# First layer of a two-layer decoder on one core: lag products moved to ScalarE, rounding to VectorE, and a selection loop without instructions that read two SBUF tensors

## The reference, cut to what matters

```python
def reference(x, ctx_768, masks, weights):           # x (2,512,128), ctx (2,154,96)
    # layer 0, gated recurrence, then a cross attention that steers a state-space filter
    x = layernorm(x + attn0(x))
    Q, K, V = (x @ Wq), (ctx @ Wk), (ctx @ Wv)         # 4 heads of 32
    scores = einsum('bthd,bghd->bhtg', Q, K) / sqrt(32)          # 154 keys
    topv, topi = top_k(scores, 32)
    attn = zeros_like(scores).at[..., topi].set(softmax(topv))
    c_t = attn.mean(heads) @ V * text_mask
    scale_in, shift_in   = split(c_t @ W_film_in  + b_film_in)
    scale_out, shift_out = split(c_t @ W_film_out + b_film_out)
    u = layernorm(x) * (1 + gate * scale_in) + gate * shift_in
    # filter taps of 512 lags: K[d,l] = 2 Re sum_n dC[d,n] exp(dt A[d,n] l), 64 states n
    y = irfft(rfft(u) * rfft(K)) + u * D_skip
    y = y * (1 + gate * scale_out) + gate * shift_out
    x = layernorm(x + y + ffn(layernorm(x + y)))
    # layer 0 experts, then layer 1 (attention of 16 heads, cross attention, experts): not touched
```

## Time and profile before

| what | value |
| --- | --- |
| median of 3 runs | 851.5 us (851.27 to 851.51) |
| the profiled execution: its own time | 854.57 us |
| its span, first to last instruction | 852.7 us |
| busy in the span: PE, DVE, ACT, POOL | 732.2, 491.8, 274.5, 241.7 us |
| mean granted TensorE clock | 0.914 of full speed |

### The profile page before, as it was taken

One profiled execution on the slowest core, in us unless ns is written; L12 is line 12 of the kernel. 1 busy time (PEld: TensorE's weight loads), 2 busy tenths in 40 slices (PEclk: granted clock), 3 DMA queues, 4 the chain that ended last, 5 costly groups with the idle time before them and its releaser, 6 DMA issues.

```text
span 852.7 us, 8489 instructions
## 1 busy us (share of the span) xinstructions
PE 732.2 (86%) x3088; PEld 370.2 (43%) x3088; DVE 491.8 (58%) x1200; ACT 274.5 (32%) x483; POOL 241.7 (28%) x138
## 2 busy tenths in 40 slices
PE   7533556888999899999999999998996999999996
PEld 4211324548568453332222222222843244556555
DVE  7699976804405358656676776764465455332333
ACT  6446645320020210135444444443021402221220
POOL 4881750100001000205554545465071500000000
PEclk9756678987977989999999999999997989999999
DMA  7100004000200000000000000000050000000000
GB/s 293 29 0 0 0 0 172 28 1 1 98 1 1 0 1 0 2 0 1 1 0 1 1 0 1 1 0 1 1 210 0 1 1 0 1 1 0 1 1 25
DMA packets 3491, 18.64 MB, mean 22 GB/s; under 512 B 887, under 2 KB 2040, under 8 KB 2938
## 3 DMA queue, kind: packets, MB, share of 16 engines
q1 hardware_dynamic: 3450, 18.11, 5.6%
HBM read 17.58 MB, written 0.52 MB: 21 GB/s over the span
## 4 chain that ended last, share of the span: by engine, by line
PE 67%; DVE 20%; ACT 6%; issue 3%; POOL 3%; POOLq 0%; DVEq 0%; ACTq 0%
PE PS L1849 9%; PE PS L1332 7%; PE PS L1863 5%; DVE SB L1486 5%; PE PS L1316 4%; PE PS L1287 4%; PE PS L218 3%; PE PS L1300 2%; PE PS L707 2%; DVE SB L1235 2%; PE PS L1348 2%; PE PS L972 2%; PE PS L1370 2%; PE PS L1415 2%; PE PS L1647 2%
## 5 line engine op out<-in xcount | busy, mean ns | idle before, releaser
L198 POOL TENSOR_TENSOR SB<-SB 128x4 f32<-128x4 f32 (+1 forms) x24 | 23.9, 998 | 376.3 <-DVE SB L182 376.2
L1469 POOL TENSOR_TENSOR SB<-SB 128x1024 f32<-128x1024 f32 x32 | 75.3, 2354 | 127.6 <-ACT SB L1439 127.5
L1486 DVE TENSOR_REDUCE SB<-PS 128x2 f32<-128x1024 f32 x64 | 78.5, 1226 | 52.7 <-PE PS L1300 52.6
L1439 ACT ACTIVATE SB<-PS 128x1024 f32<-128x1024 f32 x64 | 65.6, 1026 | 105.2 <-PE PS L1319 105.1
L218 PE MATMUL PS<-SB 128*128 128x512 f32 (+1 forms) x190 | 87.3, 606 | 8.3 <-ACT SB L541 6.8
L1849 PE MATMUL PS<-SB 128*128 128x512 f32 x176 | 82.5, 607 | 0.0
L1316 PE MATMUL PS<-SB 64*128 64x512 f32 x256 | 68.9, 615 | 0.0
L1332 PE MATMUL PS<-SB 128*64 128x512 f32 x256 | 67.8, 610 | 1.2 <-DVE SB L1523 1.2
L1519 DVE RECIPROCAL SB<-PS 128x512 f32<-128x512 f32 x16 | 53.7, 3358 | 17.6 <-PE PS L1348 17.6
L1929 DVE TENSOR_TENSOR SB<-SB,PS 128x512 f32<-128x512 f32 (+1 forms) x48 | 32.9, 689 | 52.7 <-PE PS L1849 48.8
L1863 PEld LDWEIGHTS PS<-SB 128*128 128x128 f32 (+1 forms) x384 | 49.3, 190 | 18.6 <-issue 10.1
(11 more groups left out here) (359 smaller groups left out, 1219.4 us busy)
## 6 DMA issues: line engine op xcount, KB each, us to landing
SB<-exp SPq DMA_DIRECT2D x1, 4352.0 KB, 13.8
SB<-moe SPq DMA_DIRECT2D x1, 4096.0 KB, 12.9
SB<-dft SPq DMA_DIRECT2D x1, 2304.0 KB, 11.6
SB<-att SPq DMA_DIRECT2D x1, 2048.0 KB, 7.9
SB<-mix SPq DMA_DIRECT2D x1, 768.5 KB, 4.6
SB<-mix SPq DMA_DIRECT2D x1, 640.0 KB, 5.7
SB<-ssm SPq DMA_DIRECT2D x1, 602.0 KB, 6.7
SB<-lat SPq DMA_DIRECT2D x1, 585.0 KB
```

What stands on the lines that cost most here:

```text
L1439: act.activation(expd[i % 2][:, 1024 * u:1024 * u + 1024], bank(2 * (u % 2), 2), ACT.Exp).then_inc(sem("d_exp"), 1)
L1469: pool.tensor_tensor(half_sums[half], e[:, 0:1024], e[:, 1024:], ALU.add).then_inc(sem("d_half_sum"), 1)
L1486: dve.tensor_reduce(shift[i % 2][:, qt:qt + DK + 1:DK], two_heads(bank(4, 2)), AX_X, ALU.max, negate=True)\
```

## The change

- **Lag products.** `low_r` and `high_r` are no longer made by two large GpSimd multiplications but by 32 and 16 ScalarE activations, one for each lag (scale = the lag; the low ones add the quarter turn as bias).
- **Rounding** is one VectorE instruction each for the low and the high turns (+ MAGIC, - MAGIC), which replaces L429, two GpSimd passes (L436, L437) and ScalarE's two passes of L517.
- **Selection.** The negated maximum is a TENSOR_REDUCE with negate in place of a TENSOR_TENSOR; the last MATCH_REPLACE8 of a head writes to PSUM (banks 2, 3), so that `selected` reads one operand from there; VectorE makes only 1 / sum, and the mask multiplication moves to ScalarE at the head of `diagonals`.
- **Scores** of all tiles go to banks 0 and 1, each once the tile before is copied; PE issues them three tiles ahead of the gather.
- **Order on ScalarE.** FiLM inputs move behind the first exponentials, low rates to tile 0, high and low sines into one block in tile 2, the copies of the taps to tile 6 (TAPS_AT 4 to 5), the spectrum to tile 7. `normed_again` (8 activations) becomes one GpSimd multiplication.
- **Taps' transform** on PE directly behind gather and FiLM of tile 5, into banks 0 and 1, once all scores are copied.

```diff
-    def b_pool_turns(pool, follow):
-        pool.wait_ge(sem("s_stack_in"), 1)
-        pool.tensor_tensor(lag(low_r, LOW), every(turn_T, LOW), lags(ssm["low_lags"], LOW), ALU.mult).then_inc(sem("s_low_products"), 1)
+    def b_act_low_turns(act, a, z):
+        for l in range(a, z):
+            ins = act.activation(lag(low_r, LOW)[:, :, l], turn_T, ACT.Identity, scale=float(l), bias=ssm["quarter"])
+        if z == LOW:
+            ins.then_inc(sem("s_low_products"), 1)
+    def b_act_high_turns(act, a, z):
+        for l in range(a, z):
+            ins = act.activation(lag(high_r, HIGH)[:, :, l], turn_T, ACT.Copy, scale=float(LOW * l))
+        if z == HIGH:
+            ins.then_inc(sem("s_high_turns"), 1)
...
+    def b_dve_rounds(dve):
         dve.wait_ge(sem("s_low_products"), 1)
-        dve.tensor_scalar(low_k, low_r, ssm["quarter"], MAGIC, ALU.add, ALU.add).then_inc(sem("s_low_rounds"), 1)
+        dve.tensor_scalar(low_k, low_r, MAGIC, MAGIC, ALU.add, ALU.subtract).then_inc(sem("s_rounds"), 1)
+        dve.wait_ge(sem("s_high_turns"), 1)
+        dve.tensor_scalar(high_t, high_r, MAGIC, MAGIC, ALU.add, ALU.subtract).then_inc(sem("s_rounds"), 1)
-    def b_pool_high_turns(pool, follow):
-        follow(pool.tensor_tensor(lag(high_r, HIGH), every(turn_T, HIGH), lags(ssm["high_lags"], HIGH), ALU.mult))
-        m = magic[:, 0:1].to_broadcast([P, 2048])
-        pool.wait_ge(sem("a_out"), 2)
-        follow(pool.tensor_tensor(high_t, high_r, m, ALU.add))
-        follow(pool.tensor_tensor(high_t, high_t, m, ALU.subtract))
+    def b_pool_high_angles(pool):
+        pool.wait_ge(sem("s_rounds"), 2)
         pool.tensor_tensor(high_t, high_t, high_r, ALU.subtract).then_inc(sem("s_high_turns"), 1)
...
     def b_act_pre(act):
-        b_act_low_rates(act, 0, 8)
+        b_act_low_turns(act, 0, 24)
         for h in range(H_X):
             act.wait_ge(sem("x_inputs"), h + 1)
...
-        b_act_low_rates(act, 8, 12)
+        b_act_low_turns(act, 24, LOW)
+        b_act_high_turns(act, 0, 10)
+        act.wait_ge(sem("x_half_turned"), 1)
+        act.activation(xsT[:, 0:512], bank(4), ACT.Copy).then_inc(sem("x_half_in"), 1)
+        b_act_high_turns(act, 10, HIGH)
+        act.wait_ge(sem("turned"), 1)
+        act.activation(xsT[:, 512:], bank(5), ACT.Copy).then_inc(sem("turned_in"), 1)
...
-    TAPS_AT = 4
+    TAPS_AT = 5
...
         def score(t):
-            if t >= 2:
-                pe.wait_ge(sem("x_scores_in"), t - 1)
-            else:
-                pe.wait_ge(sem("x_small_in"), (2, 6)[t])
+            if t >= 1:
+                pe.wait_ge(sem("x_scores_in"), t)
...
-                o = bank(2 * (t % 2) + g)[:, 0:2 * S2]
+                o = bank(g)[:, 0:2 * S2]
...
         def peak(j):
-            dve.tensor_tensor(minus_max[:, 2 * j:2 * j + 2], peaks.rearrange("p (i m) -> p i m", m=8)[:, 2 * j:2 * j + 2, 0],
-                              minus_one, ALU.mult).then_inc(sem("x_minus_max"), 1)
+            dve.tensor_reduce(minus_max[:, 2 * j:2 * j + 2], peaks[:, 16 * j:16 * j + 16].rearrange("p (i m) -> p i m", m=8),
+                              AX_X, ALU.max, negate=True).then_inc(sem("x_minus_max"), 1)
...
-                    ins = dve.match_replace(left[i % 4], m8[k][:, 8 * r:8 * r + 8], left[i % 4], 0.0)
+                    to = rest[:, S2 * k:S2 * k + S2] if r == 3 else left[i % 4]
+                    ins = dve.match_replace(to, m8[k][:, 8 * r:8 * r + 8], left[i % 4], 0.0)
...
-                              left_ring[:, S2 * (i % 4):S2 * (i % 4) + 2 * S2], ALU.subtract).then_inc(sem("x_probs"), 1)
+                              bank(2 + j % 2)[:, 0:2 * S2], ALU.subtract).then_inc(sem("x_probs"), 1)
...
-            follow(dve.reciprocal(a, sums))
-            dve.tensor_tensor(a, a, text_mask[:, t:t + 1].to_broadcast([P, H_X]), ALU.mult).then_inc(sem("x_share"), 1)
+            dve.reciprocal(sums, sums).then_inc(sem("x_sums"), 1)
...
     def b_act_attention(act):
...
         exponentials(0)
+        b_act_film_inputs(act)
         exponentials(1)
-        b_act_low_whole(act)
+        b_act_film_rows(act)
         for t in range(NT):
             if t >= 1:
                 diagonals(t - 1)
+            if t == NT - 1:
+                b_act_spectrum(act)
             if t + 1 < NT:
                 exponentials(2 * t + 2)
             if t + 2 < NT:
                 scores_in(t + 2)
+            if t == 0:
+                b_act_low_rates(act, 0, 16)
+            if t == 2:
+                b_act_high_waves(act)
+                b_act_low_waves(act)
+            if t == TAPS_AT + 1:
+                b_act_taps(act)
             if t + 1 < NT:
                 exponentials(2 * t + 3)
-            if t == TAPS_AT + 1:
-                b_act_taps(act)
             if t >= 1:
                 attn_in(act, t - 1)
                 for k in FILMS[t - 1]:
                     film_in(k)
             if t == 0:
-                b_act_low_rates(act, 20, LOW)
-            if t == 1:
-                b_act_high_waves(act)
-            if t == 2:
-                b_act_low_waves(act)
+                b_act_low_rates(act, 16, LOW)
             if t == 3:
                 b_act_high_rates(act)
-                normed_again()
-            if t == 6:
-                b_act_spectrum(act)
```

More of the change, by code:

```diff
@@ L477, in b_act_spectrum @@
         w = lambda j: ssm["bin_weight"][:, j:j + 1]
-        for out, i in ((taps_re, 6), (taps_im2, 7), (taps_re2, 6)):
+        for out, i in ((taps_re, 0), (taps_im2, 1), (taps_re2, 0)):
             for j in range(4):
@@ L510, in b_act_high_rates @@
         ins.then_inc(sem("s_rates"), 1)
[L512 to L517, removed]
     def b_act_high_waves(act):
-        act.wait_ge(sem("s_high_turns"), 1)
+        act.wait_ge(sem("s_high_turns"), 2)
         act.activation(high_r, high_t, ACT.Abs).then_inc(sem("s_high_waves"), 1)
@@ L530, in b_act_low_waves @@
             act.wait_ge(sem("s_low_products"), h + 2)
-            act.activation(low_k[:, c], low_k[:, c], ACT.Sin, scale=-TWO_PI, bias=ssm["quarter_angle"])\
+            act.activation(low_k[:, c], low_k[:, c], ACT.Sin, scale=-TWO_PI)\
                .then_inc(sem("s_low_waves"), 1)
@@ L724, in film_tile, with taps_spectrum @@
                       stop=True).then_inc(sem("x_film"), 1)
+        def taps_spectrum():
+            pe.wait_ge(sem("x_scores_in"), NT)
+            pe.wait_ge(sem("s_taps_in"), 1)
+            pe.wait_ge(sem("dft_in"), 16)
+            for part, mat in ((0, dft["dft_cos"]), (1, dft["dft_sin"])):
+                for j in range(4):
+                    for c in range(4):
+                        ins = pe.matmul(bank(part)[:, 128 * j:128 * j + 128],
+                                        mat[:, 512 * c + 128 * j:512 * c + 128 * j + 128],
+                                        taps[:, 128 * c:128 * c + 128], start=(c == 0), stop=(c == 3))
+            ins.then_inc(sem("s_taps_dft"), 1)
         score(0)
         score(1)
+        score(2)
         for t in range(NT):
-            if t + 2 < NT and t < TAPS_AT:
-                score(t + 2)
+            if t + 3 < NT:
+                score(t + 3)
             if t == TAPS_AT:
-                score(t + 2)
-                score(t + 3)
                 taps_of_lags()
@@ L744, in b_pe_attention @@
                 film_tile(k)
-            if t == 5:
-                pe.wait_ge(sem("x_film_in"), 5)
-                pe.wait_ge(sem("s_taps_in"), 1)
-                pe.wait_ge(sem("dft_in"), 16)
-                for part, mat in ((0, dft["dft_cos"]), (1, dft["dft_sin"])):
-                    for j in range(4):
-                        for c in range(4):
-                            ins = pe.matmul(bank(6 + part)[:, 128 * j:128 * j + 128],
-                                            mat[:, 512 * c + 128 * j:512 * c + 128 * j + 128],
-                                            taps[:, 128 * c:128 * c + 128], start=(c == 0), stop=(c == 3))
-                ins.then_inc(sem("s_taps_dft"), 1)
+            if t == TAPS_AT:
+                taps_spectrum()
         pe.wait_ge(sem("s_u_late"), 1)
@@ L781, in select @@
             base = 12 * j
+            rest = bank(2 + j % 2)[:, 0:2 * S2]
             if j >= 2:
@@ L850, in diagonals @@
         def diagonals(t):
+            act.wait_ge(sem("x_sums"), 2 * t + 2)
+            act.activation(share[:, H_X * t:H_X * t + H_X], total[:, H_X * t:H_X * t + H_X], ACT.Copy, scale=text_mask[:, t:t + 1])\
+               .then_inc(sem("x_share"), 1)
             act.wait_ge(sem("x_share"), t + 1)
@@ L862, in film_in @@
             act.activation(film[:, 512 * t:512 * t + 512], bank(6 + t % 2), ACT.Copy).then_inc(sem("x_film_in"), 1)
-        def normed_again():
-            act.wait_ge(sem("u_scaled"), 1)
-            for t in range(NT):
-                ins = act.activation(tiled(u_n)[:, t, :], tiled(xs)[:, t, :], ACT.Copy, scale=u_scale[:, t:t + 1])
-            ins.then_inc(sem("u_normed"), 1)
         scores_in(0)
```

45 lines of the change are left out of this document (18 added, 27 removed).

## The result

The kernel after takes **799.8 us** median (798.87 to 800.62, 4 executions) against 851.5 (851.27 to 852.36) before: ratio 0.9391, 95% interval 0.9374 to 0.9407. The profiled execution took 798.87, its span 797.0 us, at a mean granted clock of 0.947 (0.914 before).

A forecast was written before the change was run, and what follows sets the result against it. It took the chain through VectorE, ScalarE and PE up to the last FiLM copy as the bound; gains 13.6 + 12.9 + 12.4 = 38.9 take 854.57 to 815.7, less 3.1 for the median: 812.6 us, range 803 to 824.

The forecast's parts named there:

- Locks: VectorE against GpSimd: GpSimd keeps VectorE out only where it reads two SBUF tensors; L314 would fall to 0.69 us.
- Rival (d): VectorE: GpSimd keeps out any VectorE instruction, so only the order pays (about 14 + 4); 833 us, chance 0.02.
- rival (e): Selection: MATCH_REPLACE8 into PSUM is slow, 28 of them at 2 us each make the kernel slower; 869 us, chance 0.02.
- Part 1: Up to the first selection: its start moves from 51.6 to 38.0 us, a gain of 13.6.
- Part 2: From the first selection to the taps: 81.0 us becomes 68.1, a gain of 12.9.
- Both stalls: VectorE waits before the taps: 2.5 us for exponentials 7 behind the sines, 2.3 us for the scores of tile 6.
- gather 3 94.3, FiLM 2 97.0, ... gather 4 102.9, FiLM 3 105.6: Predicted end times in us of PE's gathers and FiLM tiles just ahead of the taps, which start at 106.1.
- Part 3: From the taps to the last FiLM copy: 57.3 us becomes 44.9, a gain of 12.4.
- what follows is the same code: Behind the last FiLM copy: nothing the change touches, so everything there only shifts by the same amount.
- a falling clock behind 151: Filter stage after the last FiLM copy: a falling granted clock, partly giving back the 39 us, would show the forecast wrong.
- Rival (c): Before the taps: waits shrink, PE high early (3), block hidden (2.5), gathers high (1.9 per tile); 801 to 806 us, chance 0.10.
- The step from the profile to the median: Whole kernel: the median lies 3.1 us below the profiled execution, so 815.7 becomes 812.6.

The follow-up runs named there:

- c: The kernel after run once more, unchanged, in more rounds; median 799.1 us.
- e6: The kernel after with scores issued two tiles ahead of the gather and not three; 832.9 us.
- e7: The kernel after with the sines in two blocks, high ones at the end of tile 1, low ones at the end of tile 2; 809.7 us.
- e4: The kernel before with PE's two idle stretches filled by unused matmuls, six behind the taps and four behind the transform; 838.1 us.
- e15: The kernel before with the negated maximum by TENSOR_REDUCE and the mask multiplication on ScalarE, subtraction unchanged; 846.4 us.
- e9: The kernel after with three unused VectorE multiplications (2.2 us) ahead of the second half of u, PE idle meanwhile; 807.6 us.
- e3: The kernel after with eight unused VectorE multiplications (5.8 us) ahead of the second half of u, PE idle meanwhile; 809.4 us.
- e10: The kernel after with eleven unused VectorE multiplications (7.9 us) ahead of the second half of u, PE idle meanwhile; 806.1 us.
- e8: The kernel after with six unused matmuls in PE's idle stretch beside the copies of the taps; 799.6 us.
- e5: The kernel after with eight unused VectorE multiplications (5.8 us) ahead of the second half of u, PE doing seven unused matmuls meanwhile; 813.5 us.

## Why the prediction was right, and where it was wrong

**Locks: right.** That only two SBUF inputs are kept out, that L312 would take 0.69, the negated maximum and the subtraction their plain time, and that a PSUM write costs nothing, all came out (9 ns for the write). Rival (d) and rival (e) are refuted by the groups (171, 472 and 314 ns). The rounding did keep GpSimd out (2.75 us beside it) and cost nothing. The 1.0 us that the PSUM figure of the page "VectorE: DVE Perf Modes" of the Trainium skill (section on the TRN2 errata) would have added did not appear: a subtraction takes 472 ns, where an undisturbed one before took 470 to 480.

**Part 1: right, 0.7 too late.** A lag at 0.29, ScalarE free at 27.2, xsT at 27.8, all as worked out; the first scores ran half at the upper level (30.4 for 31.3), tile 1's at the lower.

**Part 2: the mechanism right, a term mis-sized.** Both stalls stand where they were put, 2.5 us for exponentials 7 at 74.4 (75.0 forecast), and 0.85 for the scores of tile 6 at 90.2 (2.3, at 92.0). The step that failed is "gather 3 94.3, FiLM 2 97.0, ... gather 4 102.9, FiLM 3 105.6": it priced gathers at 3.8 and the tiles behind at 2.7, the lower level of before. In the kernel after both gathers took 2.1 at most and both FiLM tiles 2.1, which is 4.6 us less. Gather 2 and FiLM 1, priced at 3.8 and 3.0, took 3.5 and 2.1, another 1.2, and the block of sines ended 0.6 early; against that gather 4 stood 0.65 us behind the scores of tile 7 and a matmul that nothing uses. Together that makes up the 5.5 us by which the taps came early, to within 0.3. Which gathers run high is not settled by the pause ahead of them: behind 2.8 us of idle time gather 3 ran high in the kernel after and low in c, where the first scores ran high, and the taps start at the same time in both. So what was mis-sized is how much of PE's work up to the taps runs at the upper level.

**Part 3: right.** 44.3 against 44.9. No run takes its edits singly (TAPS_AT 5, the transform's new place, the spectrum behind `diagonals(6)`); e6 and e7 show what it costs if the clock falls at the taps: 5 to 6.6 us.

**The sum: the step "what follows is the same code" failed.** It carried 662.9 over unchanged, and it was 652.1. The prediction named a falling clock behind 151 as a sign of being wrong and gave a rising one no place. The rows of before would have warned: at 243.00 to 262.50 the granted clock is 0.56 with PE busy all the time, 7.7 us that another course of the clock could return. Rival (c), PE high early, was the true direction; it was bounded by the changed part alone, and so was the low end of the range, 803. With up to 11 us of the part behind added, the range would have reached 792 and held 799.8. The step from the profile to the median was off the other way: it took 3.1 us off, and the median after lies 0.9 above its profiled execution. So the 12.8 us by which the forecast was missed are 6.1 ahead of the last FiLM copy and 10.8 behind it, less these 4.0, to within 0.1.

**Of the 55.7 us between the two profiles:** 44.9 lie in the changed part. Taken singly inside the new order, and always up to the taps, the locks are 12.2, the third tile ahead 29.5, one block of sines 6.7, lags off GpSimd 8.9. They sum to 57.3 where the whole change brings 31.9 up to there, so they overlap; in the old order two of the three lock edits are 8.5. The other 10.8 are granted clock, and e4 gains 10.6 in that part without the change.

**Left open:** by what the chip grants the clock. Between 211 and 243 us before, and between 162 and 194 after, PE does the same work at the same distances (49.5 us apart throughout), both at 1.00; right behind it the clock falls in the one and not in the other. So PE's work in that stretch does not tell the two apart, and since five profiles with last FiLM copies up to 18.8 us apart have the same part behind within 0.2 us, lateness alone does not either. No run here separates PE's work further back from the chip's own course, by which six executions of c differ by 10.7 us.

## What to carry to other kernels

A small instruction that takes microseconds names a resource, not its own work: find what runs beside it, and compare it with a neighbour of another operand placement. When a stall is taken away, follow what is late next, engine by engine: with two of the three locks gone but the old order kept, VectorE's wait for scores grew from 15.0 to 28.5 us (e15). Where a long part behind the change holds stretches at the lower clock, put them into the range: a change that does not touch them can return or take them.

## What the runs showed of the hardware that was not expected

- One program, unchanged, spreads over 10.7 us (795.06 to 805.78, c) and follows its mean granted clock. A difference of 1% between two single executions says nothing without it.
- The same 64 matmuls of 64 columns take 7.33 or 13.89 us, and 12.34 also behind 14 us of unbroken work (e7). The same half of a gather behind the same pause of 2.8 us takes 1.13 (after) or 1.99 (c).
- Idle time of 4.3 to 10.2 us just ahead of the filter went each time with 1.5 to 2.1 us more in its first 96 matmuls (e9, e3, e10), but so did a pause of 2.1 in e8.
- Work without use on PE can cost more than idleness over the rest of the program: 659.9 with, 656.7 without (e5, e3, one profile each, both less the delay; medians 813.5 and 809.4).
